# Attention and experts kernel: value products after every third score pair, the splits of three operands handed to POOL

## The reference

```python
result = (embeddings @ w_qkv).reshape(b, s, 3, 16, 8)      # q, k, v by head
scores = einsum('bnqd,bnkd->bnqk', q, k) / sqrt(128)
probs = softmax(scores, axis=-1)
ctx = einsum('bnqk,bnkd->bnqd', probs, v)
x = layernorm(x + ctx)
...
x = layernorm(x + experts(x))
```

## Time and profile before

| | |
|---|---|
| median of three runs | 750.67 us (747.97 to 754.08) |
| the profiled execution | 755.64 us, its span 754.0 us |
| attention, feed forward | to about 421 us, from there to 754 us |
| busy in the span: TensorE, VectorE, ScalarE, POOL | 92%, 71%, 56%, 34% |
| TensorE's granted clock, mean | 0.957 of full |

### The profile page before, as it was taken

The page is one execution under the profiler, slowest core; times in us unless marked ns, Lnnn a source line. Parts: engine busy times, 40 slices in busy tenths (PEclk is TensorE's granted clock), DMA queues, the critical chain, the costliest instruction groups (busy, mean ns, idle before and its releaser), DMA issues. The chain is left out here.

```text
span 754.0 us, 13194 instructions
## 1 busy us (share of the span) xinstructions
PE 690.4 (92%) x3488; PEld 356.2 (47%) x3488; DVE 533.4 (71%) x1130; ACT 423.4 (56%) x824; POOL 259.0 (34%) x281
## 2 busy tenths in 40 slices
PE   3898898989989898898889999999999999999995
PEld 1332333333333333333333566667676767666663
DVE  1989999999999999989972354556555565647343
ACT  2077878878778787788876343434342433434321
POOL 2102101111111111111110265656565666666463
PEclk8579999999999999999995699999999999999999
DMA  5832241422414223142101405050322305050500
GB/s 181 264 89 74 81 140 56 134 64 73 143 45 149 65 75 125 51 143 65 39 4 50 176 1 225 1 201 37 136 102 83 156 23 216 14 224 0 239 1 28
DMA packets 34279, 74.89 MB, mean 99 GB/s; under 512 B 4144, under 2 KB 13488, under 8 KB 30032
## 3 DMA queue, kind: packets, MB, share of 16 engines
q1 hardware_dynamic: 33440, 72.38, 28.1%
q0 software_dynamic: 816, 2.23, 0.8%
HBM read 58.61 MB, written 15.99 MB: 99 GB/s over the span
## 5 line engine op out<-in xcount | busy, mean ns | idle before, releaser
L685 ACT ACTIVATE probs<-ps_k 128x512 f32<-128x512 f32 x512 | 271.6, 607 | 87.7 <-PE ps_k L796 86.6
L728 DVE TENSOR_REDUCE maxima<-ps_bank 128x1 f32<-128x512 f32 x392 | 251.4, 682 | 25.2 <-PE ps_bank L789 19.3
L1022 POOL TENSOR_TENSOR hidden<-gated,weights 128x512 f32<-128x512 f32 x128 | 167.3, 1312 | 125.5 <-DVE gated L1104 108.9
L796 PE MATMUL ps_k<-q_aug,k_aug 32*128 32x512 f32 x512 | 162.5, 493 | 23.0 <-ACT probs L685 22.0
L1052 ACT ACTIVATE silu<-ps_gate 128x512 f32<-128x512 f32 x136 | 81.4, 599 | 178.8 <-PE ps_gate L1146 178.5
L789 PE MATMUL ps_bank<-k_aug,q_aug 32*128 32x512 f32 x392 | 156.5, 507 | 18.2 <-DMA q_aug<-q_rows 8.4
L1104 DVE TENSOR_TENSOR gated<-silu,ps_up 128x512 f32<-128x512 f32 x128 | 87.1, 685 | 108.1 <-PE ps_up L1146 73.1
L796 PEld LDWEIGHTS ps_k<-q_aug,k_aug 32*128 32x128 f32 x512 | 64.4, 186 | 175.5 <-ACT probs L685 152.9
L809 PE MATMUL ps_ctx<-probs,v_ones 128*32 128x512 f32 x1024 | 142.2, 629 | 0.1
L1171 PE MATMUL ps_y<-hidden,nets_down 128*128 128x512 f32 x272 | 137.1, 591 | 0.0
L1143 PE MATMUL ps_gate<-x1T_high,nets_low 128*128 128x512 f32 x136 | 97.1, 714 | 0.0
(11 more groups left out here) (108 smaller groups left out, 616.0 us busy)
## 6 DMA issues: line engine op xcount, KB each, us to landing
weights<-combine_rows SPq DMA_DIRECT2D x32, 1024.0 KB, 7.9
k_aug<-k_rows SPq DMA_DIRECT2D x32, 256.0 KB, 2.7
q_aug<-q_rows SPq DMA_DIRECT2D x32, 256.0 KB, 3.1
q_rows<-qk_high SPq DMA_DIRECT2D x16, 256.0 KB, 2.9
k_rows<-qk_high SPq DMA_DIRECT2D x16, 256.0 KB, 3.0
net_raw<-w_nets POOLq DMA_DIRECT2D x17, 128.0 KB, 3.1
xT_sb<-xT SPq DMA_DIRECT2D x8, 256.0 KB, 2.9
q_rows<-qk_low SPq DMA_DIRECT2D x8, 256.0 KB, 2.9
```

What stands on the lines that cost most here:

```text
L685: act.activation(probs[:, t % 2, h, :], ps_k[SCORE_SLOT[i]][:], ACT.Exp, scale=ATT_SCALE).then_inc(exp_done, 1)
L728: dve.tensor_reduce(maxima[:, parity, TILES * h + t:TILES * h + t + 1], bank("q", (i - UNIT * AHEAD) % SCORES)[:], AX_X, ALU.max).then_inc ...
L796: return pe.matmul(ps_k[SCORE_SLOT[i]][:], k_aug[rows, g, t * P:(t + 1) * P], q_aug[rows, g, :], start=True, stop=True).then_inc(scores_k, 1)
L1022: pool.tensor_tensor(hidden[:, s % RING, :], gated[:, s % UP_RING, :], r.weights[:, e, :], ALU.mult).then_inc(hidden_done, 1)
```

## The change

Four things change in the attention stage.

1. Value products stand behind pairs 8, 11, 14, 20, 23, 26, 32, 35, 41, 44, 47, 50, 56, 59, 62, and the last tile's behind pair 2 of the next batch: always at the end of three pairs. `probs` has four tiles of room and not two.
2. The small products stand at the ends of such triples too: turned maxima after 2, 17, 32, 50 (before: 2, 18, 34, 50), q and k after 5 and 11 (before 6 and 10), v after 17 (before 13), turned sums after 8 and 41 (before 25 and 57). Copies of sums on ScalarE follow exps 2 and 35 (before 4 and 36); VectorE normalises behind maximum 8 and 41.
3. The rounding and the remainder of shift rows, q and k go to POOL, two passes each. ScalarE makes only the raw copy, VectorE nothing. The first unit's shift rows and the first batch's q and k stay as they were.
4. Semaphores `qk_staged` and `shift_staged` free the bank after the raw copy.

```diff
+WINDOW = 3
+WEIGH_AFTER = weigh_after()
+MAX_AFTER = [2, 17, 32, 50]
+QK_AFTER = [5, 11]
+V_AFTER = 17
+CONTEXT_AFTER = [8, 41]
+X1_AFTER, GATE_AFTER, COMBINE_AFTER = 41, 47, 56
...
+def weigh_after():
+    after, i = [], -1
+    for tile in range(UNIT):
+        i += WINDOW * (2 if tile == UNIT // 2 else 1)
+        while i < GROUP * tile + 2 * WINDOW and i + WINDOW < SCORES:
+            i += WINDOW
+        after.append(i if tile < UNIT - 1 else SCORES + WINDOW - 1)
+    return after
...
-        probs = sb("probs", [P, 2, GROUP, SEQ])
+        probs = sb("probs", [P, TILES, GROUP, SEQ])
...
+            def split_shift(u):
+                pool.wait_ge(shift_staged, u + 1)
+                pool.wait_ge(shift_written, DMA * u)
+                pool.tensor_tensor(shift[:, 0, :], shift_raw[:], r.ones[0:GROUP * TILES, 0:P], ALU.mult
+                                   ).then_inc(shift_high, 1)
+                pool.wait_ge(shift_high, u + 1)
+                pool.tensor_tensor(shift[:, 1, :], shift_raw[:], shift[:, 0, :].bitcast(F32), ALU.subtract
+                                   ).then_inc(shift_split, 1)
+            def split_qk(b, i):
+                pool.wait_ge(qk_staged, 2 * b + i + 1)
+                pool.wait_ge(rows_written, 6 * DMA * b)
+                pool.tensor_tensor(qk_high[:, i, :], qk_raw[:, i, :], r.ones[:], ALU.mult
+                                   ).then_inc(qk_highs, 1)
+                pool.wait_ge(qk_highs, 2 * b + i + 1)
+                pool.tensor_tensor(qk_low[:, i, :], qk_raw[:, i, :], qk_high[:, i, :].bitcast(F32), ALU.subtract
+                                   ).then_inc(qk_split, 1)
...
             def body(b, first=False, last=False):      # POOL
                 for g in range(GROUPS):
                     u = GROUPS * b + g
+                    if not (last and g == GROUPS - 1):
+                        split_shift(u + 1)
                     if not (first and g == 0) and not (last and g > 0):
                         pool.wait_ge(context_step, 4 * u)
                         ...
                         place_v(u + 3, (g + 3) % GROUPS)
+                    if g == 0 and not last:
+                        split_qk(b + 1, 0)
+                        split_qk(b + 1, 1)
...
-            def round_shift(u, src, first):
+            def stage_shift(u, src):
                 act.wait_ge(maxima_turned, u + 1)
-                    act.wait_ge(shift_loaded, GROUP * DMA * u)
-                act.copy(shift_raw[:], src[0:GROUP * TILES, 0:P])
-                act.copy(shift[:, 0, :], src[0:GROUP * TILES, 0:P]).then_inc(shift_high, 1)
+                act.wait_ge(shift_split, u)
+                act.copy(shift_raw[:], src[0:GROUP * TILES, 0:P]).then_inc(shift_staged, 1)
...
-            def round_qk(b, i, src, first):
+            def stage_qk(b, i, src):
                 act.wait_ge(qk_projected, 2 * b + i + 1)
-                act.copy(qk_raw[:, i, :], src[:])
-                act.copy(qk_high[:, i, :], src[:]).then_inc(qk_highs, 1)
+                act.wait_ge(qk_split, 2 * (b - 1) + i + 1)
+                act.copy(qk_raw[:, i, :], src[:]).then_inc(qk_staged, 1)
...
-                        if t > 0:                       # TensorE
-                            weigh_values(u, g, t - 1, ...)
-                        elif begun:
-                            weigh_values(u - 1, (g + 3) % GROUPS, TILES - 1, None)
+                        if i + SCORES == WEIGH_AFTER[-1] and not first:
+                            weigh_values(GROUPS * b - 1, GROUPS - 1, TILES - 1, None)
+                        if i in WEIGH_AFTER:
+                            of, t = divmod(WEIGH_AFTER.index(i), TILES)
+                            weigh_values(GROUPS * b + of, of, t, ...)
+                        if i == MAX_AFTER[g] and not (last and g == GROUPS - 1):
+                            wait_bank(("max", g), b, first, last)
+                            turn_maxima(u + 1, (g + 1) % 2, bank("max", g))
```

More of the change, by code:

```diff
@@ L48 @@
 BANKS = 4
+def weigh_after():
[13 more added lines that the diff above has]
+X1_AFTER, GATE_AFTER, COMBINE_AFTER = 41, 47, 56
 def bank_uses():
     uses = []
[L55 to L74, removed]
+    for i in range(SCORES):
+        uses.append(("q", i))
+        if i in QK_AFTER:
+            uses.append(("qk", QK_AFTER.index(i)))
+        if i == V_AFTER:
+            uses.append(("v", 0))
+        if i == X1_AFTER:
+            uses.append(("x1", 0))
+        if i in CONTEXT_AFTER:
+            uses.append(("context", CONTEXT_AFTER.index(i)))
+        if i == GATE_AFTER:
+            uses.append(("gate", 0))
+        if i == COMBINE_AFTER:
+            uses.append(("combine", 0))
+        if i in MAX_AFTER:
+            uses.append(("max", MAX_AFTER.index(i)))
     assert len(uses) % BANKS == 0
@@ L94, in used_in @@
         return not last or n < GROUPS - 1
-    return not (first and n == 1)
+    return not (first and n == 0)
 def bank_user_before(use, first, last, ahead=False):
@@ L686, in body @@
                                            scale=ATT_SCALE).then_inc(exp_done, 1)
-                            if (t, h) == (0, 3) and not (last and g == GROUPS - 1):
-                                round_shift(u + 1, bank("max", g), False)
-                            if (t, h) == (1, 0) and g == 0 and not first:
+                            if i == 2 and not first:
                                 copy_context(2 * b - 1, True)
-                            if (t, h) == (1, 0) and g == 2:
+                            if i == 35:
@@ L692, in body @@
                                 copy_context(2 * b, not first)
-                            if (t, h) == (1, 3) and g == 0 and not last:
-                                round_qk(b + 1, 0, bank("qk", 0), False)
-                            if (t, h) == (2, 3) and g == 0 and not last:
-                                round_qk(b + 1, 1, bank("qk", 1), False)
-                            if (g, t, h) == (2, 2, 1) and last:
+                            if i == QK_AFTER[0] and not last:
+                                stage_qk(b + 1, 0, bank("qk", 0))
@@ L699, in body @@
+                            if i == QK_AFTER[1] and not last:
+                                stage_qk(b + 1, 1, bank("qk", 1))
+                            if i == V_AFTER and not last:
+                                stage_v(b + 1, bank("v", 0), False)
+                            if i == MAX_AFTER[g] and not (last and g == GROUPS - 1):
+                                stage_shift(u + 1, bank("max", g))
+                            if i == X1_AFTER and last:
                                 copy_x1T(act, r, bank("x1", 0), 0, True)
-                            if (g, t, h) == (2, 2, 3) and last:
+                            if i == X1_AFTER + 1 and last:
@@ L701, in body @@
                                 act.wait_ge(r.x1T_ready, 1)
                                 round_x1T(act, r)
-                            if (g, t, h) == (2, 3, 3) and last:
+                            if i == GATE_AFTER and last:
                                 decay_gates(act, r, bank("gate", 0), 0)
-                            if (g, t, h) == (3, 1, 3) and last:
+                            if i == COMBINE_AFTER and last:
                                 copy_combine(act, r, bank("combine", 0), 0, True)
-                            if (t, h) == (3, 2) and g == 0 and not last:
-                                stage_v(b + 1, bank("v", 0), False)
@@ L710, in _ @@
-            round_qk(0, 0, c.ps_turned, True)
-            round_qk(0, 1, ps_ctx, True)
+            first_qk(0, c.ps_turned)
+            first_qk(1, ps_ctx)
             stage_v(0, ps_k[0], True)
-            round_shift(0, bank("max", GROUPS - 1), True)
+            first_shift(bank("max", GROUPS - 1))
             body(0, first=True)
@@ L809, in weigh_values @@
                     last = pe.matmul(ps_ctx[32 * h:32 * (h + 1), :], v_ones[:, g, t, h, :],
-                                     probs[:, t % 2, h, :], start=opens, stop=closes)
+                                     probs[:, t, h, :], start=opens, stop=closes)
                 last.then_inc(context_step, 1)
```

139 lines of the change are left out of this document (67 added, 72 removed).

## The result

The changed kernel took a median of **749.27 us** in 20 runs (741.69 to 752.5), against 753.95 us for the kernel before in 20 runs beside it (747.97 to 760.01). The ratio is 0.9922, 95% interval 0.9893 to 0.9951. The change makes the kernel faster by 0.8%, where 3.2% was forecast; the time lies above the range of 711 to 743. The profiled execution took 750.2 us with a span of 748.5; the one before had 755.64 and 754.0. So a difference of 5.5 us between two spans has to be explained, where the sum had 24.3.

A forecast was written before the change was run, and what follows sets the result against it. Attention was taken as bound by the ring through three slots, with VectorE close behind. Savings of 21.4 (loop), -0.6 (first batch), 1.2 and 2.3 (last) made 24.3, taking 750.67 to 726 us; forecast 718 to 733, range 711 to 743.

The forecast's parts named there:

- The loop: Six equal attention batches between first and last: 3.57 us saved in each, 21.4 in all.
- The middle batch of 43.0: One loop batch falls from 46.57 to 43.0 us: VectorE busy 40.4 plus 2.6 of losses.
- The single loss behind pair 11: k's projection waits there for the normalisation, a value product follows: VectorE loses 0.9 us a batch.
- rival 1: Ring's waits come back elsewhere, behind copies of sums and at banks 5, 11, 17: batch 44.8, total 738 us; 18%.
- The product starts within a run of weighing triples: In the loop, value products in successive triples start 1.8 us apart, where they were 2.7.
- The first batch: POOL's two nets delay the third unit's shift rows: gain 3.6, loss 4.2, net 0.6 us longer.
- The last batch: First two units save 1.2 us, last two 2.3 if the clock falls at the same place.
- POOL's prices: In each batch, a 128x512 pass on POOL takes 1.31 us and one of 128 columns 0.46.
- rival 5: POOL's new work holds VectorE's maxima: 5.3 us a batch, about 780 us in all; 2%.
- Rival 4: k's chain through POOL delays the head of the third unit in every batch: slower, 771 us; 6%.
- The work off VectorE: Four shift subtracts and two 128x512 subtracts leave VectorE per batch: 2.5 us.
- Rival 3: Nearly nothing: rival 1, and the third unit late by 1 to 2 us in each batch: 747 us; 8%.

The follow-up runs named there:

- experiment 10: Changed kernel with nets 0 and 1 split on POOL before the first batch and turned sums after pairs 29 and 53: 740.53 us, ratio 0.984.
- experiment 4: Order of the kernel before, with the roundings and remainders of shift rows, q and k on POOL: 760.08 us, ratio 1.0097.
- 9: Order of the kernel before, roundings and remainders on POOL, nets 0 and 1 split there before the first batch: 749.11 us, ratio 0.9943.
- experiment 7: Changed kernel with nets 0 and 1 split before the first batch and the first turned sums after pair 14, not 8: 736.54 us, ratio 0.9765.
- experiment 1: Changed kernel with nets 0 and 1 split on POOL before the first batch, not inside it: 742.36 us, ratio 0.987.
- 11: Changed kernel, nets 0 and 1 split before the first batch, turned sums after 29 and 53, an extra product before pair 39: 739.5 us, ratio 0.982.
- 12: Changed kernel, nets 0 and 1 first, turned sums after 14 and 41, extra products before pairs 30, 39, 54 in the last batch only: 740.9 us, ratio 0.9858.
- experiment 8: Changed kernel, nets 0 and 1 first, value product of the third unit's first tile after pair 38, not 41: 753.52 us, ratio 0.9872.
- experiment 6: Changed kernel, nets 0 and 1 first, nine extra 128-row products of 0.50 us a batch, three in each of three gaps: 767.7 us, ratio 1.019.

## Why the prediction was wrong

**The loop: 21.4 forecast, 6.3 seen.** Two steps failed, and together they are the missing 15.

- *The middle batch of 43.0 was mis-sized.* Undisturbed it is 44.21. VectorE's busy time was put at 40.4 and is 40.85; its idle at 2.6 and is 3.36 (44.21 - 40.85), above the kernel before's 3.24. The single loss behind pair 11 was put at 0.9 and is 0.88. The rest is small waits of 0.2 to 0.5 spread over the batch, where three bounds lie within 0.02 of one another per triple; that is rival 1 in small. The product starts within a run of weighing triples, forecast 1.8 apart, are 1.66 to 2.06 apart in this batch, 1.87 on average. 6 x 1.2 = 7.2 us.
- *The clock was taken as full inside the loop.* The prediction counted its fall in the last batch alone. Spreading products over triples puts six pairs between some of them, and in the profile there are six falls of 3.4 us. Six undisturbed batches would have saved 6 x (46.57 - 44.21) = 14.2, and 6.3 were saved: the falls cost 7.9 us. In all profiles of kernels with the new order, each fall in the loop begins inside the gap between products 26 and 32, 35 and 41, or 50 and 56, or behind the start of the product that ends it, by at most 1.2 us (in experiment 10 by up to 2.1). The gaps of six pairs from 2 to 8 and from 14 to 20 have the projections of q and v in them, and no fall in the loop. In the last batch, which has no projections, the clock does fall there: at 379.5, in the product behind pair 20 (379.04). With products after every fourth pair (the kernel before, experiments 4 and 9) no loop batch had one.

The 20 runs agree with that price. Four took 741.69 to 742.33 at a clock of 0.957, three 751.1 to 752.5 at 0.941. A difference of 0.016 over 748.5 us is the loss of seven falls (0.016 x 748.5 / (0.5 x 3.4)), and 9.5 us over seven is 1.36 each. The four fast ones are then near the 742 of an almost undisturbed loop. That is an estimate, as these runs left no trace of where their clock fell. The spread alone does not point at the loop: the kernel before, with no fall in its profiled loop, spreads as widely (747.97 to 760.01).

The Trainium skill, "TensorE: Matmul & The Clock Gate", section "HAM oscillation — how this bites in real kernels", puts falls in mid-kernel down to gaps in which TensorE is idle between bursts. Here TensorE was busy 2.30 of the 2.70 us before the fall at 120.1, and no idle piece in it is over 0.40 us; by that section this loop would have kept its clock, and the measurement decides. The same page of the Trainium skill, section "A second HAM failure mode: psum-queue depth-cycling", comes nearer: short idle pieces between groups of products, as the banks go round. But the kernel before has such a piece in each plain tile (0.45) and no fall in its loop.

**The first batch: -0.6 forecast, -4.1 seen.** The wait itself was forecast rightly: late at the third unit because of two loads of nets, reads landed at 68, scores at 68.38. Two things were missed. Behind the standstill of 5.57 us (4 forecast) the clock is at half for 6.8 us (30.7 in experiment 4), for which the sum had nothing: the queue's price is 6.6 by experiment 7, and 4.2 was counted. And the gain of a loop batch, 3.6, was credited to this one too. The first unit runs at half clock until 47 to 53 us, whatever the kernel. Experiment 7, free of the queue and at full clock from 47.9, gained 2.5 (46.75 against 49.21). 2.5 - 6.6 is the -4.1 seen.

**The last batch: 3.5 forecast, 0.8 seen.** The condition was "if the clock falls at the same place". It did not. It fell earlier and in pieces: 379.5, 393.2 and 406.8, for 17 us in all where it had been 27.3 in one (from 398.7). The third unit took 15.76 (13.77 before) and the fourth 11.91 (14.21 before): 0.3 saved where 2.3 was counted. The first two units saved 0.5 where 1.2 was counted.

**Behind the last exp: 0 forecast, 3.9 seen.** Nobody forecast this. The half clock of before reached to 426.0, past the last exp at 417.2, and the work behind it ran in it. After, the clock is full from 413.6 on. In every profile in which the clock is full from the last exp until the last 10 us of the span, this work takes 333.0 us, as it does here and in experiments 1, 7 and 9; in the kernel before it took 336.8. So this gain hangs on where the last fall of attention happens to end. It came by luck and not by the mechanism of the prediction.

**What was right.** POOL's prices (1.28 and 0.447 against 1.31 and 0.46) were right, and the reductions pay nothing for them, as forecast: 683 ns, as before, with POOL twice as busy. The Trainium skill, "SBUF — State Buffer", section "Who interferes with whom", has it that way and the trace agrees; so rival 5 is out. Rival 4 is out: in the loop the second unit's shift write is issued at 155.10, 9.5 us after the end of maximum 8 (145.62), and the reads at 157.66, and the third unit starts without a wait. The work off VectorE was 2.48 a batch (43.33 to 40.85) against 2.5.

**Rival 3** (nearly nothing, 747) came nearest in time, but not in cause: no third unit was late in the loop. None of the rivals was the mechanism that decided: no rival had the clock fall inside the loop.

**Open**: what decides whether a given gap brings a fall. Experiments 1 and 7 show the same work with and without, and so do the batches of one profile: two falls, one and none in turn. The gaps of the new order are needed for the falls seen in the loop, but they are not enough: the profiles of 7, 11 and 12 have them and no fall there. The gap can't be closed by placing products alone, since `probs` of a tile must be complete; moving tile 8 to 38 only moved it, and came with longer falls elsewhere.

## What to carry to other kernels

Before the distance between TensorE's large products is stretched, and after, read the granted clock by stretch through the whole loop, not its mean, and price a fall (here 1.3 us) against what the stretching saves (here 1.0 a batch). Two changes that each relieve one of two close bounds should be tried together and each alone: here 2.4 against 1.0 and 0.9. And work handed to an engine with idle time stands in that engine's list: what had waited there for a load at no cost (two nets, 3.4 to 6.6 us in the first batch) is now ahead of it and belongs elsewhere.

## What the runs showed of the hardware that was not expected

- The granted clock fell to half (1.2 GHz) in the middle of a loop in which TensorE is busy 95% of the time (41.88 of 44.21 us), for 3.4 us in most cases. The longest fall in any loop here is 20.5 us (experiment 8). No idle piece of TensorE is over 0.45 us in the stretches shown before the falls, save 0.68 in experiment 6.
- The same instructions at the same distances brought a fall in one execution and none in another (292.0 of experiment 1, 291.4 of experiment 7).
- Three products of 128 rows and 0.50 us each between the scores, in a stretch with an idle piece of 0.68 us, did not keep the clock (129.0 of experiment 6).
- POOL's passes of two inputs and VectorE's reductions run side by side at no cost to the reductions: 15.76 us of POOL in a batch, reductions at 683 ns.
